# Latent attention in a two-layer kernel: the fourth key tile of both heads also summed from fp16 halves, and loads issued in another order

## The chip, the cores and the metric

The kernel runs on one core of a Trainium2 chip. The core has five engines that run side by side and meet only at semaphores: TensorE (PE, with PEld for its weight loads), VectorE (DVE), ScalarE (ACT), GpSimd (POOL) and SyncE (SP), whose queue issues nearly all DMAs here. The metric is the device time of the program in microseconds (us), where lower is better.

## The reference, cut to what matters

Two transformer layers with adaptive norms run over x of shape 2 x 512 x 512. Nearly all that the change touches is the attention of the second layer, which has 128 heads of width 4, a latent of 64 and a rope part of 64:

```python
q_c = (c_q @ Wq_up).reshape(b, s, N_HEADS, HEAD_DIM)       # 128 heads, width 4
q_r = (x @ Wq_rope).reshape(b, s, N_HEADS, ROPE)           # width 64
k_c = (c_kv @ Wk_up).reshape(b, s, N_HEADS, HEAD_DIM)
v_c = (c_kv @ Wv_up).reshape(b, s, N_HEADS, HEAD_DIM)
k_r = x @ Wk_rope                                          # shared by the heads
scores = (einsum('bqhd,bkhd->bhqk', q_c, k_c) + einsum('bqhd,bkd->bhqk', q_r, k_r)) / scale
attn = softmax(scores, axis=-1)
out = einsum('bhqk,bkhd->bqhd', attn, v_c)                 # then @ Wo
```

All is float32, and the kernel keeps close to that accuracy by splitting values into a high and a low part.

## The kernel before, in words

The second layer's attention is cut into 128 units (`UNITS`): a unit is one pair of heads in one of the two batches, so even and odd units alternate between the batches. Scores stand with keys on partitions: 512 keys are four tiles of 128, two heads make eight slots of 128 keys x 512 queries. `SLOTS` gives their order: slots 0, 1, 4, 6 are tiles 0 to 3 of head 0 and slots 2, 3, 5, 7 those of head 1.

The engines run one software pipeline over turns u. In turn u:

- **TensorE** makes the scores of unit u, one slot after another (`scores1_rope` L2584, `scores1_content` L2591, into banks 0 to 3, slot s in bank s % 4); a second set of scores of unit u+2 for its row maxima (`max_scores` L2569, eight matmuls with queries on partitions, into banks 4 and 5 in turn); the rope queries of unit u+3 (L2499 to L2501, twelve matmuls); and `sum_unit` of unit u-1, the sum of exponentials times values. The order is written out in `before_sums` and `behind_sums`: slots 0 to 3 with maxima 0 and 1, the sums, then slot 4, maximum 2, rope, maximum 3, slot 5, rope, maximum 4, slot 6, rope, maximum 5, slot 7, maximum 6, rope, maximum 7.
- **VectorE** reduces each maximum bank (L1925, eight a turn), transposes them (L1937) and makes the low part of the rope queries (L1877, L1878). Maximum i may start on TensorE once reduction i-2 is done (`max_done`), since two banks serve eight.
- **ScalarE** evacuates the rope queries (L1364, L1365) and takes the exponentials of the eight slots (L1404) into `PT`, which is `x` for even units and `pT` for odd ones.
- **GpSimd** prepares the values (L896 to L906) and, each second turn, the low part of rope weights (L841), whose high part is a cast on VectorE (L1798).
- **SyncE** issues the loads of one turn in a fixed order (`period`): key rows k2 of unit u+1 (L569), key rows km of unit u+3 (L576), query rows q2 of unit u+3 (L580), a copy q1 of unit u+2 (L587), weights and stores each second turn (L529, L600), the row of maxima of unit u+2 (L616). A `hold` in front of each is the wait on the buffer.

For units below `HALVED` = 96 the exponentials of some slots are split into two fp16 halves, so that the sums can be fp16 matmuls with values in three bf16 parts. With `HTILES` = 3 these are the slots of tiles 0 to 2, six of eight. GpSimd makes both halves of slots 0 and 1 and the low halves of slots 2 and 3 (`halve`, L914, L916, L925), ScalarE the high halves of slots 2 and 3 (L1415). Slots 4 and 5 (`IN_PLACE`) keep their exponential in the PSUM bank, where ScalarE copies the high half (L1411) and VectorE subtracts the low half (`unit_low`, L1916, counted by `p_low`); the bank is free for the next unit's slot only after that. The sums are then twelve fp16 matmuls of 512 columns (L2614; the four column groups of the array, head x half, run side by side, so four make a round) and for the fourth tile four fp32 matmuls of 256 columns (L2619), each recorded as two. Units 96 to 127 use fp32 sums only (L2624).

Of the kernel before, what the change touches and what calls it, by code (L numbers as in the profile page):

```python
# [48 lines left out]
HTILES = 3  # L49
IN_PLACE = (4, 5)  # L50
# [21 lines left out]
def adaln_two_layers(nc, a, out):  # L72
# [8 lines left out]
    with ctx:  # L81
# [175 lines left out]
        halved_part = lambda par, s, i: pH[:, par, s, i] if s < 4 else pH_late[:, par, s - 4, i]  # L257
# [177 lines left out]
        def _(sp):  # L435
# [126 lines left out]

            def period(u, k):

                v, vb = u + 1, (k + 1) % 2
                if exists(v, UNITS):
                    hold(scores1, 8 * (v - 1))
                    for h in range(2):
                        sp.dma_start(k2[rows(h), vb, h].bitcast(F32), key_rows(kc_d[vb, hd(u, k, 1, h)]))\  # L569
                          .then_inc(k2c_loaded[vb], 16)  # L570

                v, vb = u + 3, (k + 3) % 2
                if exists(v, UNITS):
                    hold(max_mm, 8 * (v - 1))
                    for h in range(2):
                        sp.dma_start(km[rows(h), vb, h].bitcast(F32), key_rows(kc_d[vb, hd(u, k, 3, h)]))\  # L576
                          .then_inc(mc_loaded[vb], 16)
                    hold(scores1, 8 * (v - 3))
                    for h in range(2):
                        sp.dma_start(q2[rows(h), (k + 3) % 4, h].bitcast(F32), query_rows(qc_d[vb, hd(u, k, 3, h)])).then_inc(mc_loaded[vb], 16)  # L580
# [31 lines left out]
                if exists(v, UNITS):  # L612
                    hold(m_turned, v + 1)
                    for h in range(2):
                        r = maxrow(h)
                        sp.dma_start(q2[r:r + 1, (k + 2) % 4, h].bitcast(F32).rearrange("p (q n) -> p q n", q=4),  # L616
                                     mrow[h:P:32, k % 2]).then_inc(m_loaded[k % 2], 16)
# [16 lines left out]
            for b in range(B):  # L634
                for h in range(2):
                    sp.dma_start(k2[maxrow(h):maxrow(h) + 1, b, h].bitcast(F32), ost[0:1, 0]).then_inc(rope_loaded, 16)
            period(-3, 1)
            store_content(0, (1,))
            for i in range(2, 4):
                sp.wait_ge(c_stored[i], CONTENT_DMAS[i % 2])  # L640
            for u in range(-2, 6):
                period(u, u % 4)
                if u == -2:
                    store_content(2)
# [66 lines left out]
        def _(pool):  # L711
# [131 lines left out]
            def zero_others():  # L843

                pool.wait_ge(f_added, NT)
                pool.memset(ost[0:1, 0], 1.0).then_inc(zeroed, 1)
                pool.memset(vp[:], 0.0).then_inc(zeroed, 1)
                pool.memset(mcol[:].bitcast(F32), 0.0).then_inc(zeroed, 1)
                pool.wait_ge(zeroed, 3)
                for kp in range(2):  # L850
                    ones = slice(OROWS * kp + DEN, OROWS * kp + DEN + HD1)
                    pool.memset(vp[:, kp, HTILES:TB, :, ones], 1.0).then_inc(zeroed, 1)
                    pool.memset(vpb[:, kp, 0:HTILES, :, ones], 1.0).then_inc(zeroed, 1)

# [33 lines left out]
            def values(v, k, pair):  # L888
# [8 lines left out]
                pool.tensor_copy(vp[:, kp, HTILES:TB, :, OROWS * kp:OROWS * kp + HD1], full[:, HTILES:TB])  # L897
# [10 lines left out]
            def halve(u, k, pair):  # L908

                par = k % 2  # L910
                for i in range(2):
                    pool.wait_ge(exp1, 8 * u + 5 + i)
                    pool.sem_inc(spare, 1)
                    pool.tensor_copy(halved_part(par, i, 0), PT[par][:, i]).then_inc(p_split, 1)  # L914
                    pool.wait_ge(p_split, 4 * u + i + 1)
                    e = pool.tensor_tensor(halved_part(par, i, 1), PT[par][:, i], halved_part(par, i, 0), ALU.subtract)  # L916
                    if i == 1:
                        e.then_inc(p_split, 1)
# [7 lines left out]
                e.then_inc(p_split, 1)  # L926
# [6 lines left out]
            pool.wait_ge(zeroed, 7)  # L933
# [568 lines left out]
        def _(dve):  # L1502
# [367 lines left out]
            dve.wait_ge(zeroed, 7)  # L1870
# [270 lines left out]
        def _(pe):  # L2141
# [429 lines left out]
            def scores1_rope(u, k, s, use):  # L2571

                if exists(u, UNITS):
# [7 lines left out]
                    if s + 4 in IN_PLACE and exists(u - 1, HALVED):  # L2581
                        pe.wait_ge(p_low, 2 * u - 1 + s)
# [10 lines left out]
            def sum_unit(w, k, pair):  # L2593

                if exists(w, UNITS):
# [12 lines left out]
                    if halved:  # L2608
                        pe.wait_ge(p_split, 4 * w + 4)
                        pe.wait_ge(p_low, 2 * w + 2)  # L2610
                        for kb in range(HTILES):
                            for h in range(2):
                                for half in range(2):
                                    pe.matmul(rows(2 * h + half), vpb[:, k % 2, kb, h], halved_part(k % 2, SLOTS.index((h, kb)), half),  # L2614
                                              start=(kb == 0 and opens), stop=False)
                        for h in range(2):
                            for half in range(2):
                                at = slice(half * S // 2, (half + 1) * S // 2)
                                e = pe.matmul(rows(2 * h + half)[:, at], vp[:, k % 2, HTILES, h], PT[k % 2][:, SLOTS.index((h, HTILES)), at],  # L2619
                                              start=False, stop=closes)  # L2620
# [296 lines left out]
```

## Time and profile before

| | us |
|---|---|
| median of three runs | 2191.26 (2188.32 to 2196.27) |
| the profiled execution | 2196.99 |
| its span | 2195.2 |
| busy in the span: PE / DVE / ACT / POOL | 2137.4 / 1732.2 / 1345.1 / 1357.9 |

The span of the profile begins at 0. The first layer fills about the first 740 us, the turns with halves lie from about 821 to 1775 us, the turns with fp32 sums up to about 2098 us, and an output projection and the last feed-forward end the program. In a row of the timeline the first number is the start, the second the busy time of the row (for "x2" both instructions together, which may overlap), and a bracket at the end gives the idle time before it and what ended that. TensorE's matmuls overlap in the records: one lasts 0.39 us, but the next starts 0.23 us after it.

### The profile page before, as it was taken

Reading aid. Unit: us, or ns where it says so; the run is one execution under the profiler, and the core shown is the slowest. Engines: PE = TensorE matmul, PEld = TensorE weight load, DVE = VectorE, ACT = ScalarE, POOL = GpSimd, SP = SyncE. Lnnn points to the kernel's source line nnn. Section 1 sums busy time; section 2 is a strip of 40 time slices with the busy share of each in tenths; the row PEclk is TensorE's granted clock in tenths of the full one; section 3 lists DMA queues with packets and bytes.
Section 4 is the critical chain, followed back from the end, with each engine's and each line's share of the span. In section 5 each row is a group of like instructions: output and inputs, shape, how many; then the busy total and the mean of one; then the engine's idle time right before and its main releaser. Section 6 shows DMA issues by size and latency. Waiting matters only on the chain.

```text
span 2195.2 us, 42822 instructions
## 1 busy us (share of the span) xinstructions
PE 2137.4 (97%) x11276; PEld 1646.2 (75%) x11276; DVE 1732.2 (79%) x3095; ACT 1345.1 (61%) x2709; POOL 1357.9 (62%) x1621
## 2 busy tenths in 40 slices
PE   7999999999999989999999999999999999999978
PEld 4788888888886757777777777777777777777756
DVE  6788788788786748888888888888888877788764
ACT  2443443443433568888888888888888865555542
POOL 4766766766763447777777777777777721354333
PEclk9999999999999999999999999999999999999999
DMA  7011010010013143222222222222222222444441
GB/s 247 20 49 30 19 48 29 19 48 29 19 25 115 47 177 108 77 66 76 74 77 65 76 78 72 70 71 78 73 74 67 77 77 81 133 131 120 114 129 39
DMA packets 138991, 165.82 MB, mean 76 GB/s; under 512 B 30261, under 2 KB 72917, under 8 KB 138916
## 3 DMA queue, kind: packets, MB, share of 16 engines
q1 hardware_dynamic: 135076, 152.31, 24.1%
q0 software_dynamic: 3840, 12.59, 1.9%
q8 instruction: 37, 0.61, 0.1%
q14 instruction: 38, 0.31, 0.0%
HBM read 101.52 MB, written 29.10 MB: 60 GB/s over the span
## 4 chain that ended last, share of the span: by engine, by line
PE 81%; DVE 8%; SPq 3%; issue 3%; DMA 2%; ACT 1%; POOL 1%; DVEq 0%; ACTq 0%; POOLq 0%
PE bank L2584 11%; PE bank L2569 10%; PE bank L2591 10%; PE bank L2146 7%; PE bank L2148 6%; PE bank L2147 6%; PE bank L2501 5%; PE bank L2499 5%; PE bank L2500 5%; PE bank L2614 3%; PE bank L2624 3%; PE bank L2619 2%; DMA q<-qc_d 1%; DVE rope_b L1622 1%; DVE rope_a L1621 1%
## 5 line engine op out<-in xcount | busy, mean ns | idle before, releaser
L1925 DVE TENSOR_REDUCE mcol<-bank 128x1 fp32r<-128x512 f32 x1024 | 683.7, 687 | 199.5 <-PE bank L2569 189.1
L2569 PE MATMUL bank<-km,q 128*128 128x512 f32 x1024 | 412.6, 404 | 9.2 <-ACT q L1365 5.0
L2584 PE MATMUL bank<-q,k 128*128 128x512 f32 x1024 | 417.9, 408 | 0.1
L2591 PE MATMUL bank<-q,k 128*128 128x512 f32 x1024 | 404.2, 395 | 0.0
L2569 PEld LDWEIGHTS bank<-km,q 128*128 128x128 f32 x1024 | 317.6, 310 | 69.3 <-issue 16.0
L1404 ACT ACTIVATE pT<-bank 128x512 f32<-128x512 f32 x416 | 228.8, 601 | 114.5 <-PE bank L2591 112.3
L1404 ACT ACTIVATE x<-bank 128x512 f32<-128x512 f32 x416 | 228.5, 601 | 90.0 <-PE bank L2591 87.5
L2584 PEld LDWEIGHTS bank<-q,k 128*128 128x128 f32 x1024 | 192.3, 188 | 85.3 <-issue 40.4
L2591 PEld LDWEIGHTS bank<-q,k 128*128 128x128 f32 x1024 | 193.4, 189 | 31.7
L2501 PE MATMUL bank<-hT_hi,wr_lo 128*128 128x512 f32 x512 | 205.4, 401 | 0.0
L2499 PE MATMUL bank<-hT_hi,wr_hi 128*128 128x512 f32 x512 | 202.2, 395 | 0.1
L2500 PE MATMUL bank<-hT_lo,wr_hi 128*128 128x512 f32 x512 | 202.2, 395 | 0.0
L841 POOL TENSOR_TENSOR wr_lo<-wst,wr_hi 128x512 fp32r<-128x512 f32 x64 | 82.5, 1289 | 132.5 <-DVE wr_hi L1798 132.5
L2146 PE MATMUL bank<-hT_hi,w_hi 128*128 128x512 f32 x376 | 150.9, 401 | 0.0
L2148 PE MATMUL bank<-hT_hi,w_lo 128*128 128x512 f32 x376 | 148.9, 396 | 0.0
L2147 PE MATMUL bank<-hT_lo,w_hi 128*128 128x512 f32 x376 | 148.8, 396 | 0.0
L914 POOL CAST pH<-x 128x512 f16<-128x512 f32 x96 | 58.8, 613 | 126.0 <-ACT x L1404 126.0
L735 POOL TENSOR_TENSOR bq_lo<-rope_a,bq_hi 128x512 fp32r<-128x512 f32 x64 | 83.3, 1303 | 82.0 <-ACT bq_hi L1136 82.0
L727 POOL TENSOR_TENSOR rope_a<-rope_a,rope_b 128x512 f32<-128x512 f32 x80 | 105.5, 1320 | 43.9 <-DVE rope_b L1623 43.9
L1916 DVE TENSOR_TENSOR pH_late<-bank,pH_late 128x512 f16<-128x512 f32 x192 | 131.1, 683 | 1.5
L1404 ACT ACTIVATE bank<-bank 128x512 f32<-128x512 f32 x192 | 112.0, 583 | 27.6 <-PE bank L2591 26.9
L916 POOL TENSOR_TENSOR pH<-x,pH 128x512 f16<-128x512 f32 x96 | 117.6, 1225 | 7.7
(372 smaller groups left out, 5066.5 us busy)
## 6 DMA issues: line engine op xcount, KB each, us to landing
q<-q SPq DMA_DIRECT2D x256, 128.0 KB, 2.7
wst<-in_L_attn_Wq_rope SPq DMA_DIRECT2D x64, 256.0 KB, 3.2
o_d<-ost SPq DMA_DIRECT2D x63, 256.0 KB, 3.1
st_q<-in_L_attn_wq SPq DMA_DIRECT2D x8, 1024.0 KB, 7.8
st_wo<-in_L_attn_wo SPq DMA_DIRECT2D x8, 1024.0 KB, 5.1
km<-kc_d SPq DMA_DIRECT2D x256, 32.0 KB
q<-qc_d SPq DMA_DIRECT2D x256, 32.0 KB
k<-kc_d SPq DMA_DIRECT2D x256, 32.0 KB
```

Of the source, the lines that this page charges most:

```text
L1404: act.activation(bank[s % 4][:] if in_place else PT[k % 2][:, s], bank[s % 4][:], ACT.Exp, scale=float((HD1 + ROPE) ** -0.5)).then_inc(exp ...
L1916: dve.tensor_tensor(halved_part(k % 2, s, 1), bank[s % 4][:], halved_part(k % 2, s, 0), ALU.subtract).then_inc(p_low, 1)
L1925: dve.tensor_reduce(mcol[:, k % 2, i % 4, i // 4:i // 4 + 1], bank[4 + i % 2][:], AX.X, ALU.max, negate=True)\
L2146: pe.matmul(ps, lh_, rh, start=(i == 0), stop=False)
L2147: pe.matmul(ps, lh_, rl, start=False, stop=False)
L2148: e = pe.matmul(ps, ll, rh, start=False, stop=(i == n - 1))
L2499: pe.matmul(bank[6][:], wr_hi[:, par, kk], hT_hi[:, kk, at], start=(kk == 0), stop=False)
L2500: pe.matmul(bank[6][:], wr_hi[:, par, kk], hT_lo[:, kk, at], start=False, stop=False)
L2501: e = pe.matmul(bank[6][:], wr_lo[:, par, kk], hT_hi[:, kk, at], start=False, stop=(kk == KT - 1))
L2569: pe.matmul(bank[4 + i % 2][:], q2[:, k % 4, h, i % 4:S:4], km[:, b, h], start=True, stop=True).then_inc(max_mm, 1)
L2584: pe.matmul(bank[s % 4][:], k1[:, k % 2, t], q1[:, k % 4, h], start=True, stop=False)
L2591: pe.matmul(bank[s % 4][:], k2[:, k % 2, h, t], q2[:, k % 4, h], start=False, stop=True).then_inc(scores1, 1)
```

## The change

`HTILES` becomes 4 and `IN_PLACE` gets slot 6. So all eight slots of units 0 to 95 are split. Slot 6 (head 0, fourth tile) goes the way of slots 4 and 5: ScalarE copies its high half out of PSUM, VectorE subtracts the low half. Slot 7 (head 1, fourth tile) keeps its exponential in `PT`, and GpSimd makes both halves at the end of `halve`. The halves of slots 6 and 7 lie in the room of slots 4 and 5 of `PT`, which the in-place slots leave free. `sum_unit` has sixteen fp16 matmuls of 512 columns and no fp32 ones. The small copy L897 goes. On SyncE, k2 is loaded for unit u+2 and q2 for unit u+4, both after the scores of unit u, ahead of the row of maxima.

```diff
-HTILES = 3
-IN_PLACE = (4, 5)
+HTILES = 4
+IN_PLACE = (4, 5, 6)
-        halved_part = lambda par, s, i: pH[:, par, s, i] if s < 4 else pH_late[:, par, s - 4, i]
+        halved_part = lambda par, s, i: (
+            pH[:, par, s, i] if s < 4 else pH_late[:, par, s - 4, i] if s < 6
+            else PT[par][:, s - 2].bitcast(F16)[:, i * S:(i + 1) * S])
...
+            def load_queries(u, k, ahead):
+                vb = (k + ahead) % 2
+                for h in range(2):
+                    sp.dma_start(q2[rows(h), (k + ahead) % 4, h].bitcast(F32), query_rows(qc_d[vb, hd(u, k, ahead, h)])).then_inc(mc_loaded[vb], 16)
             def period(u, k):
-                v, vb = u + 1, (k + 1) % 2
-                if exists(v, UNITS):
-                    hold(scores1, 8 * (v - 1))
-                    for h in range(2):
-                        sp.dma_start(k2[rows(h), vb, h].bitcast(F32), key_rows(kc_d[vb, hd(u, k, 1, h)]))\
-                          .then_inc(k2c_loaded[vb], 16)
...
-                    hold(scores1, 8 * (v - 3))
-                    for h in range(2):
-                        sp.dma_start(q2[rows(h), (k + 3) % 4, h].bitcast(F32), query_rows(qc_d[vb, hd(u, k, 3, h)])).then_inc(mc_loaded[vb], 16)
...
                 v = u + 2
                 if exists(v, UNITS):
+                    hold(scores1, 8 * (v - 1))
+                    for h in range(2):
+                        sp.dma_start(k2[rows(h), k % 2, h].bitcast(F32), key_rows(kc_d[k % 2, hd(u, k, 2, h)]))\
+                          .then_inc(k2c_loaded[k % 2], 16)
+                if exists(u + 4, UNITS) and not (isinstance(u, int) and u < -2):
+                    if isinstance(u, int) and u < 0:
+                        hold(max_mm, 8 * (u + 2) + 1)
+                    else:
+                        hold(scores1, 8 * (u + 1))
+                    load_queries(u, k, 4)
+                if exists(v, UNITS):
                     hold(m_turned, v + 1)
...
-                pool.tensor_copy(vp[:, kp, HTILES:TB, :, OROWS * kp:OROWS * kp + HD1], full[:, HTILES:TB])
...
-                e.then_inc(p_split, 1)
+                pool.wait_ge(exp1, 8 * u + 12)
+                pool.sem_inc(spare, 1)
+                pool.tensor_copy(halved_part(par, 7, 0), PT[par][:, 7]).then_inc(p_split, 1)
+                pool.wait_ge(p_split, 5 * u + 4)
+                pool.tensor_tensor(halved_part(par, 7, 1), PT[par][:, 7], halved_part(par, 7, 0), ALU.subtract).then_inc(p_split, 1)
...
-                        pe.wait_ge(p_low, 2 * u - 1 + s)
+                        pe.wait_ge(p_low, 3 * u - 2 + s)
...
-                        pe.wait_ge(p_split, 4 * w + 4)
-                        pe.wait_ge(p_low, 2 * w + 2)
+                        pe.wait_ge(p_split, 5 * w + 5)
+                        pe.wait_ge(p_low, 3 * w + 3)
...
-                                    pe.matmul(rows(2 * h + half), vpb[:, k % 2, kb, h], halved_part(k % 2, SLOTS.index((h, kb)), half),
-                                              start=(kb == 0 and opens), stop=False)
-                        for h in range(2):
-                            for half in range(2):
-                                at = slice(half * S // 2, (half + 1) * S // 2)
-                                e = pe.matmul(rows(2 * h + half)[:, at], vp[:, k % 2, HTILES, h], PT[k % 2][:, SLOTS.index((h, HTILES)), at],
-                                              start=False, stop=closes)
+                                    e = pe.matmul(rows(2 * h + half), vpb[:, k % 2, kb, h], halved_part(k % 2, SLOTS.index((h, kb)), half),
+                                                  start=(kb == 0 and opens), stop=(kb == HTILES - 1 and closes))
```

VectorE, one even turn from the rope weights' cast to the next turn's first reduction. `mcol<-bank` is a reduction of a maximum bank, `pH_late<-bank,pH_late` a low half, `q<-bank,q` the low part of the rope queries. Before:

```order
L1798 CAST wr_hi<-wst 128x512 [waits qr_mm,wr_loaded0]
L1925 TENSOR_REDUCE mcol<-bank 128x1 [waits max_mm] x3
L1916 TENSOR_TENSOR pH_late<-bank,pH_late 128x512 [waits exp1]
L1925 TENSOR_REDUCE mcol<-bank 128x1 [waits max_mm]
L1916 TENSOR_TENSOR pH_late<-bank,pH_late 128x512 [waits exp1]
L1925 TENSOR_REDUCE mcol<-bank 128x1 [waits max_mm] x2
L1937 STREAM_TRANSPOSE mrow<-mcol 128x4x32 [waits max_done]
L1877 TENSOR_TENSOR q<-bank,q 64x512 [waits q2_hi]
L1878 TENSOR_TENSOR q<-bank,q 64x512
L1925 TENSOR_REDUCE mcol<-bank 128x1 [waits max_mm,m_loaded1]
```

The same stretch of VectorE after the change, where `x<-bank,x` is the low half of slot 6:

```order
L1811 CAST wr_hi<-wst 128x512 [waits qr_mm,wr_loaded0]
L1938 TENSOR_REDUCE mcol<-bank 128x1 [waits max_mm] x3
L1929 TENSOR_TENSOR pH_late<-bank,pH_late 128x512 [waits exp1]
L1938 TENSOR_REDUCE mcol<-bank 128x1 [waits max_mm]
L1929 TENSOR_TENSOR pH_late<-bank,pH_late 128x512 [waits exp1]
L1938 TENSOR_REDUCE mcol<-bank 128x1 [waits max_mm]
L1929 TENSOR_TENSOR x<-bank,x 128x512 [waits exp1]
L1938 TENSOR_REDUCE mcol<-bank 128x1 [waits max_mm]
L1950 STREAM_TRANSPOSE mrow<-mcol 128x4x32 [waits max_done]
L1890 TENSOR_TENSOR q<-bank,q 64x512 [waits q2_hi]
L1891 TENSOR_TENSOR q<-bank,q 64x512
L1938 TENSOR_REDUCE mcol<-bank 128x1 [waits max_mm,m_loaded1]
```

One subtraction stands newly between the reductions 6 and 7; everything behind it is one instruction further back.

GpSimd, the work on one odd unit. Before:

```order
L914 CAST pH<-pT 128x512 [waits exp1]
L916 TENSOR_TENSOR pH<-pT,pH 128x512 [waits p_split]
L914 CAST pH<-pT 128x512 [waits exp1]
L916 TENSOR_TENSOR pH<-pT,pH 128x512 [waits p_split]
L896 CAST vp<-vc 128x6x4 [waits pv1]
L897 COPY vp<-vc 128x2x4
L900 TENSOR_TENSOR l_pad<-vc,vp 128x24 [waits vp_ready]
L903 CAST vp<-l_pad 128x6x4 [waits vp_ready]
L906 TENSOR_TENSOR vp<-l_pad,vp 128x6x4 [waits vp_ready]
L925 TENSOR_TENSOR pH<-pT,pH 128x512 [waits exp1]
L925 TENSOR_TENSOR pH<-pT,pH 128x512
```

The same work on GpSimd after the change:

```order
L923 CAST pH<-pT 128x512 [waits exp1]
L925 TENSOR_TENSOR pH<-pT,pH 128x512 [waits p_split]
L906 CAST vp<-vc 128x8x4 [waits pv1]
L909 TENSOR_TENSOR l_pad<-vc,vp 128x32 [waits vp_ready]
L912 CAST vp<-l_pad 128x8x4 [waits vp_ready]
L915 TENSOR_TENSOR vp<-l_pad,vp 128x8x4 [waits vp_ready]
L934 TENSOR_TENSOR pH<-pT,pH 128x512 [waits exp1]
L934 TENSOR_TENSOR pH<-pT,pH 128x512
L937 CAST pT<-pT 128x512 [waits exp1]
L939 TENSOR_TENSOR pT<-pT 128x512 [waits p_split]
```

The copy L897 is gone, and a cast and a subtraction of 128 x 512 stand behind all that was there.

SyncE, one odd turn. Before:

```order
L569 DMA k<-kc_d 16x1x512 [waits scores1]
L569 DMA k<-kc_d 16x1x512
L576 DMA km<-kc_d 16x1x512 [waits max_mm]
L576 DMA km<-kc_d 16x1x512
L580 DMA q<-qc_d 16x1x512 [waits scores1]
L580 DMA q<-qc_d 16x1x512
L587 DMA q<-q 64x512 [waits scores1,q2_hi]
L587 DMA q<-q 64x512
L616 DMA q<-mrow 1x4x128 [waits m_turned]
L616 DMA q<-mrow 1x4x128
```

One odd turn of SyncE after the change:

```order
L576 DMA km<-kc_d 16x1x512 [waits max_mm]
L576 DMA km<-kc_d 16x1x512
L585 DMA q<-q 64x512 [waits scores1,q2_hi]
L585 DMA q<-q 64x512
L613 DMA k<-kc_d 16x1x512 [waits scores1]
L613 DMA k<-kc_d 16x1x512
L568 DMA q<-qc_d 16x1x512 [waits scores1]
L568 DMA q<-qc_d 16x1x512
L625 DMA q<-mrow 1x4x128 [waits m_turned]
L625 DMA q<-mrow 1x4x128
```

The ten DMAs of a turn are the same; the key rows k2 and the query rows q2 have moved from the front to a place ahead of the row of maxima, and belong to a unit one further on.

## Rows read from the trace of the kernel before

**Rows 1.** The page: busy time of each engine, share of the span, instructions.
```profile
PE 2137.4 (97%) x11276; PEld 1646.2 (75%) x11276; DVE 1732.2 (79%) x3095; ACT 1345.1 (61%) x2709; POOL 1357.9 (62%) x1621
```
**Rows 2.** Windows: stretch, its length, busy PE, PEld, DVE, ACT, POOL, clock, DMA.
```profile
1300.00:1400.00 100.00, 99.84 (x565) 77.05 (x564) 85.25 (x138) 82.27 (x147) 74.65 (x117) 1.00 0.27 73
```
**Rows 3.** Timeline of TensorE's matmuls, one turn.
```profile
1313.67 0.39 PE L2569 MATMUL bank<-km,q 128*128 128x512 f32 x1
...
1318.40 0.39 PE L2614 MATMUL bank<-pH_late,vp 128*32 128x512 f16 x4
1318.62 0.60 PE L2619 MATMUL bank<-pT,vp 128*32 128x256 f32 x8
1319.15 0.50 PE L2584 MATMUL bank<-q,k 128*128 128x512 f32 x1
...
1319.73 0.39 PE L2569 MATMUL bank<-km,q 128*128 128x512 f32 x1
```
**Rows 4.** Timeline of TensorE's weight loads, the same turn.
```profile
1309.72 0.31 PEld L2569 LDWEIGHTS bank<-km,q 128*128 128x128 f32 x1
...
1316.23 0.19 PEld L2584 LDWEIGHTS bank<-q,k 128*128 128x128 f32 x1
...
1319.49 0.31 PEld L2569 LDWEIGHTS bank<-km,q 128*128 128x128 f32 x1
```
**Rows 5.** Timeline of VectorE: reductions 0, 1 of two turns, and the chain.
```profile
1308.70 1.29 DVE L1925 TENSOR_REDUCE mcol<-bank 128x1 fp32r<-128x512 f32 x2
...
1314.09 0.69 DVE L1925 TENSOR_REDUCE mcol<-bank 128x1 fp32r<-128x512 f32 x1
1314.70 0.68 DVE L1916 TENSOR_TENSOR pH_late<-bank,pH_late 128x512 f16<-128x512 f32 x1
1315.30 1.28 DVE L1925 TENSOR_REDUCE mcol<-bank 128x1 fp32r<-128x512 f32 x2
1316.61 0.41 DVE L1937 STREAM_TRANSPOSE mrow<-mcol 128x128 f32<-128x128 f32 x1
1317.10 0.68 DVE L1877 TENSOR_TENSOR q<-bank,q 64x512 fp32r<-64x512 f32 x1
...
1318.53 1.29 DVE L1925 TENSOR_REDUCE mcol<-bank 128x1 fp32r<-128x512 f32 x2
1319.85 0.43 DVE L1798 CAST wr_hi<-wst 128x512 fp32r<-128x512 f32 x1
```
**Rows 6.** Timeline around a wait of TensorE for a reduction.
```profile
816.88 0.69 DVE L1925 TENSOR_REDUCE mcol<-bank 128x1 fp32r<-128x512 f32 x1 [3.59 <-PE bank L2569]
817.62 0.31 PEld L2569 LDWEIGHTS bank<-km,q 128*128 128x128 f32 x1 [0.17 <-DVE mcol L1925]
```
**Rows 7.** Timeline of ScalarE, the same turn.
```profile
1313.16 0.60 ACT L1404 ACTIVATE pT<-bank 128x512 f32<-128x512 f32 x1 [0.19 <-PE bank L2591]
1314.57 0.60 ACT L1404 ACTIVATE pT<-bank 128x512 f32<-128x512 f32 x1 [0.81 <-PE bank L2591]
```
**Rows 8.** Timeline of GpSimd: first work of an odd and an even unit.
```profile
1307.72 0.61 POOL L914 CAST pH<-pT 128x512 f16<-128x512 f32 x1 [1.14 <-ACT pT L1404]
...
1317.49 0.61 POOL L914 CAST pH<-x 128x512 f16<-128x512 f32 x1 [2.48 <-ACT x L1404]
...
1319.98 1.31 POOL L916 TENSOR_TENSOR pH<-x,pH 128x512 f16<-128x512 f32 x1
```
**Rows 9.** Instructions by line: duration in ns, min/median/max; two of them in time.
```profile
L1798 DVE CAST wr_hi<-wst x64: 426/427/1314, 773.5 to 2048.1; 128x512 fp32r<-128x512 f32 x64
L1916 DVE TENSOR_TENSOR pH_late<-bank,pH_late x192: 678/681/692, 827.7 to 1770.5; 128x512 f16<-128x512 f32 x192
...
794.01 5.16 POOL L882 TENSOR_TENSOR c_both<-x,c_both 128x512 fp32r<-128x512 f32 x4 [11.66 <-ACT x L1310]
795.49 1.31 DVE L1798 CAST wr_hi<-wst 128x512 fp32r<-128x512 f32 x1
```
**Rows 10.** Waits of TensorE: total us, times, longest.
```profile
PE bank L2569 <- DMA q<-qc_d: 1.7, 8, 0.4
```

More of the change, by code:

```diff
@@ L636, in _ @@
                     sp.dma_start(k2[maxrow(h):maxrow(h) + 1, b, h].bitcast(F32), ost[0:1, 0]).then_inc(rope_loaded, 16)
+            load_queries(-3, 1, 3)
             period(-3, 1)
@@ L640, in _ @@
                 sp.wait_ge(c_stored[i], CONTENT_DMAS[i % 2])
+            load_queries(-3, 1, 4)
             for u in range(-2, 6):
@@ L851, in zero_others @@
                     ones = slice(OROWS * kp + DEN, OROWS * kp + DEN + HD1)
-                    pool.memset(vp[:, kp, HTILES:TB, :, ones], 1.0).then_inc(zeroed, 1)
                     pool.memset(vpb[:, kp, 0:HTILES, :, ones], 1.0).then_inc(zeroed, 1)
@@ L914, in halve @@
                     pool.tensor_copy(halved_part(par, i, 0), PT[par][:, i]).then_inc(p_split, 1)
-                    pool.wait_ge(p_split, 4 * u + i + 1)
+                    pool.wait_ge(p_split, 5 * u + i + 1)
                     e = pool.tensor_tensor(halved_part(par, i, 1), PT[par][:, i], halved_part(par, i, 0), ALU.subtract)
@@ L932, in _ @@
             pool.wait_ge(vc_ready, NT)
-            pool.wait_ge(zeroed, 7)
+            pool.wait_ge(zeroed, 5)
             values(0, 0, 0)
@@ L1869, in _ @@
             key_low(1)
-            dve.wait_ge(zeroed, 7)
+            dve.wait_ge(zeroed, 5)
             dve.wait_ge(vc_ready, NT)
```

## The prediction

> **What bounds the kernel now.** I read the page's busy shares first. TensorE is busy for 97% of the span [rows 1], so what it no longer does looks like pure gain, and VectorE at 79% looks as if it had room. Then the windows, since the share is a mean over stages: in the middle of the turns with halves TensorE is busy 99.84 of 100 us at full clock (1.00, the 2.4 GHz level), VectorE 85.25, ScalarE 82.27, GpSimd 74.65 [rows 2]. The waits agree: TensorE waited for query rows eight times, 1.7 us in all [rows 10], so loads hold nothing now. Last the timelines, because the question is not how much room VectorE has but where. A turn is the distance of two weight loads for maximum 2, 1309.72 to 1319.49: 9.77 us [rows 4]. TensorE sets it.
>
> Name the loop that comes second. Matmul 5 of the maxima starts at 1313.67 [rows 3]; its reduction starts 0.42 us later, at 1314.09. From there VectorE has no gap: reduction 5, a low half, reductions 6 and 7, transpose at 1316.61, two rope subtractions from 1317.10 (0.68 us each), and at 1318.53 the next unit's reductions 0 and 1 as a pair of 1.29 us. One reduction lasts 0.69 us (the row of reduction 5), so reduction 0 ends at 1319.22 [rows 5]. Maximum 2 may not overwrite its bank before that. How soon TensorE then goes on is seen once: a reduction from 816.88 for 0.69 us ended at 817.57, and the weight load waiting for it started at 817.62, 0.05 us later [rows 6]. So the load could start at 1319.27 and did at 1319.49 [rows 4]: VectorE's chain has 0.22 us of slack in this turn, not the 1.5 us that 85% suggests. In the turn before, the pair starts at 1308.70 [rows 5] and the load at 1309.72 [rows 4]: 1309.39 + 0.05 leaves 0.28 us. The 15% of idle time lies between reductions 1 and 5, where VectorE waits for matmuls that can't come sooner, as two banks alternate.
>
> **The change part by part.**
>
> TensorE. The fp32 round of the fourth tile takes from 1318.62 to the next scores at 1319.15, 0.53 us; an fp16 round 1318.40 to 1318.62, 0.22 us [rows 3]. A fourth fp16 round in its place saves 0.31 us a turn. If part of the 0.53 us is the change of shape back to 128 x 128 rather than fp32, less goes; below, the same row bounds it at 0.1. On 96 turns that would be 10 to 30 us if TensorE stayed the bound.
>
> VectorE. One more low half a turn between reductions 6 and 7, of 0.68 us [rows 9]. Neighbours overlap, so what it adds is the distance of starts, 1314.70 to 1315.30, 0.60 us [rows 5]; I take 0.61. It lies wholly in the gapless chain. It reads slot 6's exponential and high half: those are ready, as below.
> Reduction 0 now ends at 1319.22 + 0.61 = 1319.83, the load for maximum 2 starts at 1319.88 instead of 1319.49: 0.39 us late; in the other turn 0.33. The loop is closed: from this load to matmul 5 TensorE's work is dense (1309.72 to 1313.67, 3.95 us, unchanged), and matmul 5 starts the chain again. So a turn becomes 9.77 + 0.36 = 10.13 us, and TensorE's saved 0.31 us only lengthens its wait, since the sums are not in this loop. The wait should be 0.36 + 0.31 = 0.67 us a turn, in two places: slot 2 of the next unit needs the new low half (start 1315.30 + 0.60 behind reduction 6 [rows 5], end 1316.58, so its load may start at 1316.63 and stood at 1316.23 [rows 4]), 0.40 us; the rest before maximum 2, 0.27 us. 96 turns x 0.36 = 34.6 us slower.
> Bounds of this term: if the added distance is the full 0.68 us, 0.43 x 96 = 41 us; if restarting TensorE after the wait costs another 0.1 us (its first matmul after a pause is recorded with 0.50 instead of 0.39 us [rows 3]), 10 us more; from below, if the chain had some 0.3 us of hidden slack, 6 us.
>
> ScalarE. One more copy of a high half, about 0.6 us as the exponentials. It falls between the exponentials of slots 6 and 7: the first ends at 1313.76, the second starts at 1314.57 after 0.81 us without work [rows 7]. It fits, and the exponential of slot 7 stays at 1315.17, before the low half wants it (1315.90). Nothing. If the gap were gone it would cost at most its excess, and ScalarE has 18 us idle in 100.
>
> GpSimd. A cast (0.61) and a subtraction (at most 1.31) more per unit [rows 8]; the copy that goes is not counted. The work of the odd unit ran from 1307.72 to 1317.49 - 2.48 = 1315.01, 7.3 us; that of the even one, 1.14 us of idle after it in two turns of 19.54, took 8.6 us. New: 9.2 and 10.5, 19.7 us against two turns of 20.26. It does not bound. The halves of the even unit are ready at 1317.49 + 10.5 = 1328.0; its sums would start at about 1317.95 + 10.13 + 0.40 = 1328.5. Slack 0.5 us; nothing, and if that cover goes, half of the excess per turn.
>
> The cast L1798. Every second turn VectorE casts rope weights behind reduction 1. It takes 0.427 us in the middle, but 1.31 us once, at 795.49, while GpSimd ran four subtractions without a break from 794.01 [rows 9]. Today it starts at 1319.85, in GpSimd's pause before 1319.98 [rows 5, 8]. With 0.61 us more ahead it starts at 1320.46, inside that subtraction, which would end by 1321.15 to 1321.29. If it must wait, it ends near 1321.6, reduction 2 near 1322.3, and matmul 4, which needs that bank, comes about 0.16 us late: its load would be due at 1319.88 + 2.3 = 1322.2 (the 3.95 us to matmul 5 less six matmuls of 0.23 us and the load's lead of 0.24 us). 48 x 0.16 = 7.7 us, or nothing. I take half, 4 us.
> The Trainium skill (SBUF — State Buffer, Who interferes with whom) says that a cast in a two-port mode and a GpSimd instruction exclude each other for the whole instruction; by it the sum has the 7.7 us. The same section says that a subtraction with one input in PSUM does not contend, so the new low half would stay at its length; the 192 instances before (678 to 692 ns) agree.
>
> SyncE. The DMAs are the same. The query rows come about a turn earlier, which removes waits of 1.7 us at most [rows 10]. The row of maxima is issued behind four more DMAs, some 3 us later, and is wanted a turn later. The loop has 10.13 us for what it did in 9.77. Between -2 and 0: I take 0.
>
> Start, turns 96 to 127 and end: the same work. 0.
>
> Sum: 34.6 + 4 = 38.6. The profiled execution, 2196.99 us with 2195.2 in its span, would become 2235.6; it lies 5.7 us above the median of the runs, and the prediction is for the median: 2191.3 + 38.6 = 2230.
>
> **The rivals.**
>
> A, TensorE stays the bound. VectorE's 14.75 idle us in 100 [rows 2] take up the low half. A turn becomes 9.77 - 0.31 = 9.46 us at best: 30 us faster, 2161; with only 0.1 saved 2182. For it: the busy shares, and 85.25 plus 0.68 / 9.46 = 7.2 is below 100. Against it: the gapless stretch in rows 5, ahead of the one reduction that TensorE needs.
> The Trainium skill (Perfetto Trace Analysis, Identifying the Most-Contended Engine) would have the engine of highest occupancy looked for, and warns that matmul busy share is no measure of roofline; by occupancy alone, TensorE at 97%, one would forecast A.
>
> B, the halves cancel: VectorE's chain is shorter than I read by 0.3 us or so, or the order of loads gives something back. A turn of about 9.8 us; 2191, within noise.
>
> C, GpSimd becomes the bound. If its new pair runs into VectorE's cast and its rope-weight subtraction waits for that late cast (0.43 us more), the even unit needs 10.9 us and its sums start 0 to 0.4 us late; beyond some 0.3 us that reaches maximum 2. It decides once even and odd work together exceed 20.3 us; at 20.8 the turns are 10.4, 60 us slower, 2251. Against it: 19.7 us in the sum above.
>
> D, the change does not do what it says for loads: SyncE, whose q2 and k2 now wait for scores of the running unit, becomes late with km, the one load with less room than before. A wait of 0.2 us a turn beside mine would be hidden, more would come on top. 2240.
>
> **How the numbers follow.** My forecast 0.68 (its own range 2220 to 2243), A 0.08, B 0.07, C 0.10, D 0.07. Under 0.3%, 6.6 us, two times can't be told apart here. Faster is A and a piece of B, 0.09; same the rest of B, 0.05; slower 0.86. The range leaves out A and the far end of C: 2206 to 2250.
>
> **What would show it.** Right: the wait of weight loads at the maxima (before maximum 2) for VectorE's reductions, about 0.3 us in each of 96 turns, another at slot 2 for the new low half; TensorE busy share near 93% in the middle windows; VectorE still idle 0.5 us or more before reduction 4; turns of 10.1 to 10.2 us up to unit 95. The casts at about 1.1 us instead of 0.43 would confirm that term. Wrong: turns below 9.77 us, TensorE without waits in the middle, or its wait ended by GpSimd's halves at the sums or by a DMA.

## The result and the profile after

The changed kernel takes 2209.42 us (median of five runs, 2208.07 to 2212.48), the kernel before 2188.44 us (2188.28 to 2196.27) beside it: ratio 1.0086 [1.0071, 1.0101], 19 to 21 us slower. The forecast was 2230, 39 us over the 2191.3 that it started from, with a range of 2206 to 2250: the side and the range held, the size was twice what was measured. The profiled execution of after took 2212.48 us, 2209.5 in its span; that of before 2196.99 and 2195.2.

The page of after, engines' busy time (against [rows 1]):

```profile
PE 2146.8 (97%) x10892; PEld 1623.2 (73%) x10892; DVE 1813.9 (82%) x3191; ACT 1401.7 (63%) x2805; POOL 1510.2 (68%) x1715
```

The window in the middle of the halved turns, with the columns of [rows 2]:

```profile
1300.00:1400.00 100.00, 99.00 (x516) 73.11 (x516) 92.40 (x145) 86.35 (x154) 88.91 (x122) 1.00 0.27 72
```

TensorE's busy share is 99.00, not near the 93% that the prediction named as a sign. The matmul behind a wait is recorded longer (0.60 us instead of 0.39 for the one at 1306.70) and the records overlap, so the share hides most of the waiting. The number of matmuls needs care too: a turn has 52 of them now and had 56, so 516 are 9.9 turns, and 565 before were 10.1. The clock is the same, 1.00. Two stretches of TensorE's timeline after, weight loads and matmuls (against [rows 3, 4]):

```profile
1303.55 0.19 PEld L2597 LDWEIGHTS bank<-q,k 128*128 128x128 f32 x1 [0.50 <-issue]
...
1305.15 0.61 PE L2627 MATMUL bank<-pH,vp 128*32 128x512 f16 x8
...
1305.60 0.39 PE L2627 MATMUL bank<-pH_late,vp 128*32 128x512 f16 x4
...
1305.81 0.39 PE L2627 MATMUL bank<-pT,vp 128*32 128x512 f16 x4
...
1306.13 0.50 PE L2597 MATMUL bank<-q,k 128*128 128x512 f32 x1
...
1306.68 0.31 PEld L2582 LDWEIGHTS bank<-km,q 128*128 128x128 f32 x1 [0.25 <-DVE mcol L1938]
...
1310.63 0.39 PE L2582 MATMUL bank<-km,q 128*128 128x512 f32 x1
...
1316.80 0.31 PEld L2582 LDWEIGHTS bank<-km,q 128*128 128x128 f32 x1 [0.27 <-DVE mcol L1938]
```

The two loads for maximum 2 are 10.12 us apart. TensorE stands still in the two places that were named: ahead of slot 2 (0.50) and ahead of maximum 2, there with VectorE's reduction as the releaser (0.25, 0.27). These 0.75 us are more than a turn lost, since in dense work a weight load runs ahead of its matmul: the turn is 0.35 us longer and the sums are 0.22 us shorter (below), 0.57 us together. VectorE's timeline after, the chain that they wait for (against [rows 5]):

```profile
1300.95 0.69 DVE L1938 TENSOR_REDUCE mcol<-bank 128x1 fp32r<-128x512 f32 x1
...
1302.76 0.68 DVE L1929 TENSOR_TENSOR pT<-bank,pT 128x512 f16<-128x512 f32 x1
...
1304.07 0.41 DVE L1950 STREAM_TRANSPOSE mrow<-mcol 128x128 f32<-128x128 f32 x1
...
1305.94 1.29 DVE L1938 TENSOR_REDUCE mcol<-bank 128x1 fp32r<-128x512 f32 x2
...
1307.26 1.04 DVE L1811 CAST wr_hi<-wst 128x512 fp32r<-128x512 f32 x1
...
1311.06 0.69 DVE L1938 TENSOR_REDUCE mcol<-bank 128x1 fp32r<-128x512 f32 x1
...
1316.06 2.09 DVE L1938 TENSOR_REDUCE mcol<-bank 128x1 fp32r<-128x512 f32 x3
```

The loop adds up. From the load at 1306.68 to matmul 5 at 1310.63 are 3.95 us, from there to reduction 5 at 1311.06 are 0.43, from reduction 5 to the end of reduction 0 (1316.06 + 0.69 = 1316.75) are 5.69, then 0.05 to the load: 10.12. Before, the chain was 5.13 us (1314.09 to 1319.22 in [rows 5]). It grew by 0.56, and the slack took up 0.22 of that. These are the turns of 9.77 us; not all were.

Who TensorE waits for, 860 to 1780 us, after (total, times, longest):

```profile
PEld bank L2597 <- issue: 46.8, 93, 0.5
...
PEld bank L2582 <- DVE mcol L1938: 24.9, 91, 0.3
```

**Where the time went.** A turn's length is the distance of two transposes (L1937 before, L1950 after, 128 each), worked out for each turn from their starts. Turns 36 to 43 as an example, us:

```
before     10.39  9.79  9.77  9.78 10.36  9.77  9.78  9.77
after      10.11 10.10 10.12 10.16 10.12 10.11 10.12 10.16
```

The lengths, summed by stretch in the two profiled executions:

| | before | after | after - before |
|---|---|---|---|
| to the first transpose | 802.6 | 800.4 | -2.2 |
| turns 0 to 2 | 39.4 | 38.0 | -1.4 |
| turns 3 to 95 | 920.6 | 941.4 | +20.8 |
| turns 96 to 126 | 322.7 | 320.8 | -2.0 |
| after the last transpose | 109.8 | 108.9 | -0.9 |

The 93 turns 3 to 95 have a mean of 10.123 us after. Before, 9.77 is only the commonest length: 31 of the 93 are more than 0.08 us longer (up to 0.73), and the mean is 9.899. Against 9.775 the new turns cost 93 x 0.348 = 32.4 us, about what was predicted; but 93 x 0.124 = 11.6 us of long turns disappeared, which the prediction had at nothing.

A long turn of before, TensorE and SyncE together; SPq rows are DMA issues of SyncE:

```profile
1283.34 1.37 SPq L580 DMA_DIRECT2D q<-qc_d  x2
...
1287.62 0.31 PEld L2569 LDWEIGHTS bank<-km,q 128*128 128x128 f32 x1 [0.60 <-issue]
...
1287.62 0.61 PE L2569 MATMUL bank<-km,q 128*128 128x512 f32 x1 [0.18 <-DMA q<-qc_d]
```

The chain of waits of before in that stretch has the same transfer as its longest piece:

```profile
1284.07 3.42 DMA q<-qc_d
```

The query rows, issued third in the turn, land at 1287.49, and maximum 0, the first that needs them, starts at 1287.62 after 0.60 us without a load. The matmul's row names the DMA with only 0.18 us, its weight load's row has the whole gap and no name. The waits of before, 860 to 1780 us, beside the row in [rows 10]:

```profile
PEld bank L2569 <- issue: 12.8, 30, 0.8
```

Thirty waits, 12.8 us: the long turns. After, neither this row nor a DMA is among TensorE's waits.

### The profile page after: what moved, and what is told of

It reads as the page before. It is cut to its first block, busy times and chain, and to the rows that moved or that the text cites. A ratio compares the mean times of both kernels' runs of the same rounds, so it can differ in the third digit from the quotient of the medians.

```text
span 2209.5 us, 43070 instructions
## 1 busy us (share of the span) xinstructions
PE 2146.8 (97%) x10892; PEld 1623.2 (73%) x10892; DVE 1813.9 (82%) x3191; ACT 1401.7 (63%) x2805; POOL 1510.2 (68%) x1715
## 4 chain that ended last, share of the span: by engine, by line
PE 86%; DVE 8%; issue 2%; ACT 1%; POOL 1%; SPq 1%; DMA 1%; DVEq 0%; ACTq 0%; POOLq 0%
PE bank L2597 13%; PE bank L2582 12%; PE bank L2604 11%; PE bank L2159 7%; PE bank L2161 6%; PE bank L2160 6%; PE bank L2514 5%; PE bank L2513 5%; PE bank L2512 5%; PE bank L2627 4%; PE bank L2632 3%; DVE rope_b L1635 1%; DVE rope_a L1634 1%; DVE rope_b L1636 1%; PE bank L2295 1%
## 5 line engine op out<-in xcount | busy, mean ns | idle before, releaser
L2582 PE MATMUL bank<-km,q 128*128 128x512 f32 x1024 | 426.6, 417 | 3.6 <-ACT q L1378 2.6
L1417 ACT ACTIVATE pT<-bank 128x512 f32<-128x512 f32 x368 | 199.3, 603 | 75.6 <-PE bank L2604 73.8
L1417 ACT ACTIVATE x<-bank 128x512 f32<-128x512 f32 x368 | 199.0, 602 | 51.1 <-PE bank L2604 48.9
L1417 ACT ACTIVATE bank<-bank 128x512 f32<-128x512 f32 x288 | 167.9, 583 | 66.2 <-PE bank L2604 63.3
L1424 ACT ACTIVATE pH_late<-bank 128x512 f16<-128x512 f32 x192 | 114.7, 597 | 6.1
L925 POOL TENSOR_TENSOR pH<-x,pH 128x512 f16<-128x512 f32 x96 | 111.9, 1166 | 7.7
```

The source lines that it names most:

```text
L1417: act.activation(bank[s % 4][:] if in_place else PT[k % 2][:, s], bank[s % 4][:], ACT.Exp, scale=float((HD1 + ROPE) ** -0.5)).then_inc(exp ...
L2582: pe.matmul(bank[4 + i % 2][:], q2[:, k % 4, h, i % 4:S:4], km[:, b, h], start=True, stop=True).then_inc(max_mm, 1)
```

## The experiments

Each number of the kernel before is the median beside which the experiment ran: 2191.16 for the first four, 2192.34 for the fifth and sixth, 2191.04 for the last two. Turn lengths are worked out as above.

**The loads alone.** `HTILES` stays 3, only SyncE's order is the new one:

```diff
             def period(u, k):
-                v, vb = u + 1, (k + 1) % 2
-                ... k2 of unit u + 1 at the front
...
-                ... q2 of unit u + 3 behind km
...
+                    hold(scores1, 8 * (v - 1))
+                    ... k2 of unit u + 2
+                    load_queries(u, k, 4)
                     hold(m_turned, v + 1)
```

> The new order of the loads alone, with three halved tiles as before. Theory 1 (in the trace of before one turn in three or four is 0.1 to 0.7 us longer than 9.77, because the query rows for maximum 0 come late; the new order takes these away): every turn below unit 96 lasts 9.77 us, 12 us less in turns 3 to 95 and about 2 us less in the turns behind them, so 2174 to 2177 us. Theory 2 (loads hold nothing, as the 1.7 us of recorded TensorE waits for them say; the smaller loss comes from a shorter VectorE chain): within 2 us of before.

Measured 2175.86 us (2173.97 to 2177.08), ratio 0.9925 [0.9911, 0.9939]: 15 us faster. All 93 turns are 9.77 to 9.79 us, mean 9.775; their sum is 909.1 us, 11.5 below before. The window shows a TensorE without a gap:

```profile
1300.00:1400.00 100.00, 100.00 (x571) 78.31 (x570) 86.58 (x139) 82.36 (x148) 76.04 (x117) 1.00 0.28 75
```

SyncE's issues in this kernel, about one turn:

```profile
1282.34 1.63 SPq L611 DMA_DIRECT2D k<-kc_d  x2
1284.24 1.49 SPq L566 DMA_DIRECT2D q<-qc_d  x2
1285.84 1.18 SPq L623 DMA_DIRECT2D q<-mrow  x2
1287.28 1.62 SPq L574 DMA_DIRECT2D km<-kc_d  x2
```

The query rows issued at 1284.24 are for a unit one further on, so they have a turn more to land than those issued at 1283.34 before. This is the term that was priced at nothing, shown by itself. The key rows k2 moved with them; that it is the query rows that were late is read from the waits, which name no other load.

**The halves alone.** Four tiles in halves with before's order of loads, so the same edit backwards, made to the changed kernel.

> All four tiles in halves, with the order of loads of before. Theory 1: the late query rows were worth 12 us in turns of 9.77; in turns of 10.12 the old order of loads has 0.35 us more room per turn, so most turns stay at 10.12 and it stands 0 to 4 us above the changed kernel. If the two parts add up instead, it is 12 to 14 us above it, 2222. Theory 2 (loads hold nothing): the same as the changed kernel, with turns of 10.12 and no longer ones among them. A turn list with scattered longer turns speaks for theory 1.

Measured 2216.00 us (2214.15 to 2218.30), ratio 1.0107 [1.0088, 1.0127]. Ten of 93 turns are long (10.20 to 10.47), and none with the new loads is; the mean is 10.147, against 10.123. So the two parts don't add: loads alone -15, halves alone +25, together 19 to 21. With turns of 10.12 us the old order is rarely late, and the new one is worth some 5 us (1.0107 against 1.0086; the intervals overlap, and 0 to 4 were expected). The price of the halves once loads are right is 1.0086 / 0.9925 = 1.0162, 35 us, and 941.4 - 909.1 = 32.3 us in the 93 turns, near the 34.6 that the forecast had for 96.

**A short low half.** Is it VectorE's chain, or the work as a whole? The subtraction stays in place but covers 8 of 512 columns; the sums take slot 6's high half twice, so its low part is left out of the result.

```diff
-                dve.tensor_tensor(halved_part(k % 2, s, 1), bank[s % 4][:], halved_part(k % 2, s, 0), ALU.subtract).then_inc(p_low, 1)
+                n = slice(0, 8) if s == 6 else slice(0, S)
+                dve.tensor_tensor(halved_part(k % 2, s, 1)[:, n], bank[s % 4][:, n], halved_part(k % 2, s, 0)[:, n], ALU.subtract).then_inc(p_low, 1)
```

> The changed kernel, where the low half of slot 6 is subtracted for 8 of its 512 columns only and the sums read the high half of that slot twice (the output lacks this low part). The instruction, its waits and its place stay, its 0.68 us shrinks to about 0.15. Theory (the added subtraction in VectorE's gapless chain sets the turn): a turn falls from 10.12 by up to 0.45 us until GpSimd binds: its work on an even and an odd unit takes 10.77 and 9.0 us in the trace of the changed kernel, 9.88 a turn. So turns of 9.75 to 9.9 us, 22 to 35 us below the changed kernel, 2175 to 2188. Rival (the wait of slot 2 for the release of the bank, by its semaphore and place, sets the turn, not the length of the subtraction): under 10 us.

Measured 2188.04 us (2186.33 to 2191.83), ratio 0.9984 [0.9974, 0.9994], at the upper end of what was expected and 21 to 22 us below the change. Of the chain's timeline:

```profile
1309.98 0.15 DVE L1930 TENSOR_TENSOR pT<-bank,pT 128x8 f16<-128x8 f32 x1
```

The turns alternate between 9.59 and 10.17, mean 9.888, where they were 10.12: most of the chain's price is gone, and something else is now in front. The waits, 860 to 1780 us, name who is next:

```profile
PEld bank L2628 <- issue: 47.8, 88, 0.9
...
PE bank L2628 <- POOL x L939: 24.6, 46, 0.7
```

Each second turn the sums wait for GpSimd's last halves. (Of the first row some 0.25 us a turn is no such wait: before, the same row had 21.6 us in 88.) The pair of 19.76 is GpSimd's (its 19.7 of the forecast). The short turn is near what TensorE alone would need: 9.77 less the 0.22 that its fp16 round saves, an estimate of 9.55. VectorE's chain, without the length of the low half, ends there too: at 1313.37 reduction 0 is done, and the load for maximum 2 starts at 1313.42. So three engines stand close: TensorE at about 9.55 us a turn, GpSimd at 9.88 in this order of its work, VectorE at 10.12. Rivals A and C had named real bounds, behind the first.

**The low half one place earlier.** Slot 6's low half goes ahead of reduction 6, so that slot 2 gets its bank sooner, while reduction 0 stays where it was.

```diff
                     for i in range(8):
+                        if i == 6 and exists(w - 2, HALVED):
+                            unit_low(w - 2, k - 2, 6)
                         dve.wait_ge(max_mm, 8 * w + i + 1)
...
-                        if i in IN_PLACE and exists(w - 2, HALVED):
+                        if i in (4, 5) and exists(w - 2, HALVED):
```

> The changed kernel with the low half of slot 6 one place earlier on VectorE, ahead of reduction 6. Theory (the end of reduction 0 decides when maximum 2 goes on): the 0.5 us wait before slot 2 goes or nearly goes, the wait before maximum 2 grows from 0.25 to about 0.75 us, and the turn stays at 10.1, within 3 us of the changed kernel. Rival (the wait at slot 2 is what makes the turn longer): 0.3 to 0.5 us a turn less, 30 to 48 us faster than the changed kernel.

Measured 2211.99 us (2208.78 to 2213.23), ratio 1.0083 [1.0066, 1.0100], level with the change, in turns of 10.144 on the mean. The waits, 860 to 1780 us:

```profile
PEld bank L2584 <- DVE mcol L1940: 44.3, 91, 0.7
...
PE bank L2629 <- POOL x L939: 8.4, 40, 0.3
```

The wait at slot 2 is gone (46.8 us in the changed kernel), and the turn is no shorter. The wait ahead of maximum 2 grew from 24.9 to 44.3 us, to 0.62 us in one turn and 0.33 in the next and not to 0.75 in each; in the second kind TensorE, now earlier, first waits for GpSimd's last halves at the sums. Of the two places where TensorE stood still only the one ahead of maximum 2 sets the turn.

**VectorE's chain in another order.** From unit 4 on, to take work out from between reduction 5 and the next reduction 0:

```diff
+                        if i == 0 and ahead(w):
+                            q_low(w, k)
+                        if i == 1 and ahead(w):
+                            turn_maxima(w - 1, k - 1)
+                        if i == (3 if ahead(w) else 1) and k % 2 == 0:
                             split_rope_weights(p, (k // 2 - 1) % 2, quad)
```

GpSimd's rope-weight part goes behind the values, since the cast is later; the low half of slot 6 stays one place earlier.

> All four tiles in halves, VectorE's chain written in another order from unit 4 on: the low half of slot 6 ahead of reduction 6; the two rope subtractions between reductions 0 and 1, the transpose behind reduction 1, the cast of rope weights behind reduction 3; on GpSimd the rope-weight subtraction behind the values. The work is the same. Theory (VectorE's order made the turn 10.12, GpSimd's total of 19.77 us for two units is next): turns of 9.8 to 9.9 us, level with the short low half, 2182 to 2190 us. Rival (VectorE is short of time, not of order, at 92% busy): turns stay at 10.0 or more, 2200 to 2211.

Measured 2204.35 us (2198.37 to 2206.90), ratio 1.0048 [1.0034, 1.0061]: the total missed. The halved turns came close to what was expected (mean 9.913, and GpSimd's halves are waited for again), but turns 96 to 126 took 332.4 us instead of 320.8, single ones up to 13.96: in the fp32 turns the new order costs 12 us or more (the last of them is counted 4 us short, because the transpose that marks it moved). How was not followed up.

**The same, with ScalarE making the high half of slot 7** in GpSimd's place:

```diff
-                pool.tensor_copy(halved_part(par, 7, 0), PT[par][:, 7]).then_inc(p_split, 1)
...
+                    if s == 7 and exists(u, HALVED):
+                        act.wait_ge(exp1, 8 * u + 12)
+                        act.activation(halved_part(k % 2, 7, 0), PT[k % 2][:, 7], ACT.Copy).then_inc(last_high, 1)
```

> The one before, and ScalarE instead of GpSimd makes the high half of slot 7, behind the exponential of slot 7. GpSimd's work for two units falls from 19.77 by 2 x 0.69 to 18.4 us, 9.2 a turn. Theory: the bound goes back to TensorE or to VectorE's chain, turns of 9.4 to 9.65 us, 20 to 45 us below the one before: 2140 to 2168 us, the first version with four tiles that beats the loads alone. Rival (ScalarE, at 87% of turns of 10.1, becomes late with the exponentials and so GpSimd and the scores): no better than 9.75 us a turn, 2170 to 2190.

Measured 2213.97 us (2211.45 to 2214.79), ratio 1.0096 [1.0081, 1.0111]: a miss. GpSimd is out of the way, but the halved turns are 9.87 to 10.12, mean 10.02, and turns 96 to 126 take 332.4 us again. New waits of TensorE, 860 to 1780 us:

```profile
PEld bank L2597 <- issue: 21.7, 87, 0.3
...
PEld bank L2527 <- issue: 16.7, 66, 0.3
...
PEld bank L2527 <- DVE q L1892: 4.8, 25, 0.3
```

The first is maximum 0, which needs the rope queries that ScalarE evacuates, now behind the new copy; the second is the next rope matmul, which needs the bank that VectorE's rope subtractions release, now behind reduction 0. The two together close a loop from the rope matmuls over ScalarE, maximum 0 and VectorE back to them. This is read from the order of the instructions: only the last row names a releaser, VectorE's rope subtraction. The last experiment bears it out in part.

**The order for units 8 to 97 only,** with the rope subtractions back ahead of reduction 0; the transpose behind reduction 1 and the cast behind reduction 3 stay:

```diff
-                return not isinstance(w, int) or w >= 4
+                return not isinstance(w, int) or 8 <= w < HALVED + 2
...
-                        if i == 0 and ahead(w):
-                            q_low(w, k)
```

> As the VectorE reordering before, but for units 8 to 97 only, and with the rope subtractions ahead of reduction 0 again (only the transpose goes behind reduction 1). The trace of the copy-on-ScalarE version showed a loop through the single rope bank: rope queries, ScalarE's evacuation, maximum 0, reduction 0, rope subtractions, next rope queries. Theory: with the subtractions ahead, reduction 0 ends 0.45 us earlier than in the changed kernel, which alone gives 9.67 us a turn; GpSimd's 19.77 us for two units makes it 9.88. Turns 96 to 127 as in the changed kernel. 2184 to 2190 us. Rival (the order of VectorE was not what held it): turns above 10.0, 2200 or more.

Measured 2180.48 us (2179.05 to 2186.54), ratio 0.9957 [0.9944, 0.9971]: 0.4% faster than before, and 28 us (1.0086 against 0.9957) under the change with the same work on every engine. It is also below the 2184 to 2190 of the expectation. Turns cycle through 9.68, 9.91, 9.78 and 9.82, mean 9.79 and not 9.88. (One of 12.87 and one of 7.35 stand at the two ends of the new order, where the transpose that marks a turn changes its place; no time is lost there.) The sums still wait for GpSimd, 11.2 us in all, so its bound is not a constant: two units take it 19.6 us here for 19.76 with the short low half. There a subtraction L925 that ran beside the cast L1811 (1314.00, 0.43 us) took 1.39 us instead of 1.17; here the cast stands elsewhere and all of them take 1.16 to 1.17 about 1300 to 1340. That this makes up the difference is likely, not tested.

**The last two together,** e7's order and ScalarE's copy.

> The one before with ScalarE making the high half of slot 7. GpSimd needs 9.2 us a turn. Theory: VectorE's chain binds at 9.67 us a turn, 10 us below the loads alone: 2160 to 2172 us. Rival (ScalarE's later evacuation of the rope queries delays maximum 0): 9.8 to 10.0 us a turn, 2180 to 2200.

Measured 2177.89 us (2177.36 to 2179.83), ratio 0.9943 [0.9930, 0.9956]; the 2160 to 2172 of the expectation was missed. The turns are 9.69 to 9.87, mean 9.78, where the copy on ScalarE with the rope subtractions behind reduction 0 had 10.02: their place cost 0.24 us a turn, as the loop above would have it. TensorE no longer waits for GpSimd, but in the waits, 860 to 1780 us, and in the timeline at maximum 0 stand:

```profile
PEld bank L2594 <- issue: 20.1, 87, 0.3
```

```profile
1307.07 0.59 ACT L1376 ACTIVATE q<-bank 64x512 fp32r<-64x512 f32 x1
...
1307.88 0.31 PEld L2594 LDWEIGHTS bank<-km,q 128*128 128x128 f32 x1 [0.25 <-issue]
```

ScalarE's evacuation ends at 1307.66 behind the added copy, and the load for maximum 0 stands idle for 0.25 us, about what TensorE had gained: 9.55 and 20.1 / 87 = 0.23 are the 9.78 of the turns. The row names no releaser; that it is the evacuation is the rival that the expectation named, and is argued from the order. With all its repairs the fourth tile in halves is level with the loads alone (0.9943 against 0.9925, the intervals overlap), which have the lowest median of all versions, 2175.86, and beat both kernels.

## Why the prediction was right in its side and wrong in its size

**VectorE's chain: right.** Predicted 0.36 us a turn; the turns became 10.11 to 10.12 from 9.77, and the three quantities behind it are there: 3.95 us from load to matmul 5, 0.05 from reduction to load, a chain longer by 0.56 (0.61 was taken). The two waits came where they were put: 0.50 at slot 2 for 0.40, 0.25 to 0.27 before maximum 2 for 0.27. The experiments with a short low half and with the low half moved show that the chain up to reduction 0 is the cause. Of the signs, the waits, the length of the turns and the stretched casts came; TensorE's share of 93% did not, and VectorE was idle 0.7 us before reduction 4 only in turns without a cast, and 0.17 to 0.24 us in the others.

**The loads: the step that failed.** The query rows come earlier, "which removes waits of 1.7 us at most", and then "Between -2 and 0: I take 0". The new order removed 11.6 us in turns 3 to 95 and 2.0 in turns 96 to 126, and the loads alone gave 15 us at the medians. The term of the sum that was 0 should have been about -14. The 1.7 us of [rows 10] are only the matmuls' share of the wait. The weight loads ahead of them had 12.8 us in 30 waits in the same answer, under "issue", and I had taken the row that names a DMA for all of it. A second reading would have caught it: I took one turn, 1309.72 to 1319.49, for every turn, while 93 turns in 920.6 us give 9.90.

The larger point is that the floor of 9.77 was not what before paid. The change replaces the mean of 9.90 by 10.12, so that the effect is 0.22 a turn (20.8 us in 93 turns) and not 0.36. For turns 3 to 126, 32.4 us of the chain less 13.6 of the loads leave 18.8, beside the 19 to 21 us of the medians.

**The cast: the stretch came, the cost did not.** Predicted: cast in GpSimd's subtraction, matmul 4 late by 0.16 us, half of 7.7 taken. All rope-weight casts of after, in ns (min/median/max), against the first of [rows 9]:

```profile
L1811 DVE CAST wr_hi<-wst x64: 427/983/1527, 769.9 to 2063.8; 128x512 fp32r<-128x512 f32 x64
```

Two rows of GpSimd at one of them:

```profile
1306.84 1.17 POOL L925 TENSOR_TENSOR pH<-x,pH 128x512 f16<-128x512 f32 x1
...
1308.38 1.29 POOL L852 TENSOR_TENSOR wr_lo<-wst,wr_hi 128x512 fp32r<-128x512 f32 x1 [0.36 <-DVE wr_hi L1811]
```

The cast that starts at 1307.26 lasts 1.04 us, to 0.29 us behind the end of the subtraction, and GpSimd then waits 0.36 us for it. VectorE has the time: it waits for matmul 4 anyway. Nothing is left in the turn: of turns 36 to 43 those with a stretched cast are 37, 39, 41 and 43, and 37 and 41 last 10.10 and 10.11 us like their neighbours. The 0.05 us more in each fourth turn (10.16 for 10.11) arises between the transpose and reduction 0, before the cast, and stands as well in the turns with the short low half (9.63 for 9.59), whose casts last 0.43 us. So the term of 4 us measured 0: reductions 2 and 3 follow the cast sooner than was taken, and reduction 2 ends at about 1308.9, before the load for matmul 4 is due (1306.68 + 2.3).

The Trainium skill's rule that was weighed (SBUF — State Buffer, Who interferes with whom), by which such a cast and a GpSimd instruction exclude each other, agrees but for 0.14 us: put wholly behind the subtraction, which ends at 1308.01, the cast would have lasted 0.75 + 0.43 = 1.18 us, and it lasted 1.04. The new subtraction from PSUM kept its 0.68 us, as that section says of a subtraction with an input there. By the rule's own sum (7.7 us) the forecast would have been further off, since the wait was covered.

**TensorE: direction right.** From the round of slots 4 and 5 to the next scores it was 0.75 us (1318.40 to 1319.15 in [rows 3]) and is 0.53 (1305.60 to 1306.13): 0.22 saved, between the 0.31 and 0.1 of the text. It was hidden, as said. From the last fp16 round to the next scores are 0.32 us, where rounds follow each other in 0.21 to 0.22: some 0.1 us of the old 0.53 was going back to 128 x 128.

**GpSimd and ScalarE: right at nothing.** GpSimd was 88.91 us busy in 100; the short low half shows its bound at 9.88 us a turn, 0.24 under VectorE's. ScalarE, 86.35 us busy, added no wait of TensorE either.

**Start, last turns and end:** taken as 0. Turns 96 to 126 gained 2.0 us because three turns of 11.46 to 11.90 became 10.9 to 11.1, and the loads alone give the same (320.5). Of the remaining 4.5 us, the 1.4 in turns 0 to 2 look like the loads' too: they took 39.4 and 39.5 us with the old order of loads (before, the halves alone) and 38.0 and 36.4 with the new (after, the loads alone). The rest, at the start and the end, lies in one execution of before that was 5.7 us over its median, and is not attributed.

**The rivals.** A is refuted for this change: TensorE's loop would be about 9.55, but VectorE's binds first. B's outcome (the order of loads gives something back) is what shrank the loss, with 11.6 us and not enough to cancel. C stands 0.24 us a turn behind. D is refuted: among TensorE's waits no DMA is left.

## What to carry to other kernels

List the length of every turn before pricing a change on one of them: a mean above the floor is time that a change elsewhere can give back, and it is given back only once, since a slower loop hides the same waits. Read a wait of TensorE in the rows of its weight loads as well as in those of its matmuls, the nameless ones too. Price added work by the chain that it lengthens, less the slack at that chain's end: the same work cost 35 us over the loads alone where it lengthened the chain, and 7 us (0.9957 / 0.9925) once other work had been moved off that chain.

## What was not expected of the hardware

- A stretched cast costs its own engine's chain nothing here but holds GpSimd: the medians are 983 ns after and 427 before, and GpSimd waited 16.7 us in 46 waits for it (860 to 1780 us).
- TensorE needs about 0.1 us more to go from sums on 32 columns of the array back to 128 x 128 scores than between two rounds of sums (0.32 against 0.22).
- Small transfers can nearly fill a queue: SyncE's issues take 1.2 to 1.7 us a pair, 7.9 us in a turn of before of 9.9 (from 1279.44 to 1289.32), and their order decided 15 us of the kernel.
